# Linear attention: K^T V by heads in column strips, epsilon sums on ScalarE, second statistics moved behind the splits

## What is computed

```python
Q = relu(x @ Wq.T + bq) * decay      # (b, h, n, d), d = 32
K = relu(x @ Wk.T + bk) * decay
V = x @ Wv.T + bv
KV = einsum('bhnd,bhne->bhde', K, V)
Ksum = K.sum(axis=2)
Z = 1.0 / (einsum('bhnd,bhd->bhn', Q, Ksum)[..., None] + 1e-6)
out = einsum('bhnd,bhde->bhne', Q, KV) * Z
return out @ Wo.T + bo
```

## Time and profile before

| | |
|---|---|
| median of 3 runs | 2439.28 us (2438.57 to 2439.76) |
| profiled execution | 2436.57 us, its span 2435.0 us |
| TensorE busy | 2372.1 us (97%) |
| VectorE busy | 1214.1 us (50%) |
| ScalarE busy | 824.4 us (34%) |
| GpSimd busy | 862.6 us (35%) |
| mean granted TensorE clock | 0.993 of full speed |
| linear attention in the span | about 1473 to 1957 us |

### The profile page before, as it was taken

One profiled execution on the slowest core, in us unless ns is written; L12 is line 12 of the kernel. 1 busy time (PEld: TensorE's weight loads), 2 busy tenths in 40 slices (PEclk: granted clock), 3 DMA queues, 4 the chain that ended last, 5 costly groups with the idle time before them and its releaser, 6 DMA issues. The chain is left out here.

```text
span 2435.0 us, 39858 instructions
## 1 busy us (share of the span) xinstructions
PE 2372.1 (97%) x12749; PEld 1783.5 (73%) x12749; DVE 1214.1 (50%) x2551; ACT 824.4 (34%) x1392; POOL 862.6 (35%) x1098
## 2 busy tenths in 40 slices
PE   9999999999999999999999996999999999999997
PEld 7887755555555557788888885888888888888886
DVE  4334577777777758422222207776764732222221
ACT  3222355555555543344444431011111222222221
POOL 2000256565665552233333334442425221222112
PEclk9999999999999999999999998999999999999999
DMA  8895354545445328512121104140404242222200
GB/s 285 282 300 183 109 131 111 142 119 124 118 119 137 100 86 295 139 35 52 34 52 34 40 30 160 36 172 21 152 34 153 89 109 53 52 52 52 58 29 35
DMA packets 265860, 262.55 MB, mean 108 GB/s; under 512 B 128051, under 2 KB 161843, under 8 KB 265269
## 3 DMA queue, kind: packets, MB, share of 16 engines
q1 hardware_dynamic: 250148, 218.44, 31.2%
q0 software_dynamic: 6128, 24.21, 3.2%
q10 hardware_dynamic: 9504, 18.88, 2.3%
HBM read 168.68 MB, written 92.27 MB: 107 GB/s over the span
## 5 line engine op out<-in xcount | busy, mean ns | idle before, releaser
L191 DVE CUSTOM_DVE_ANT_0 junk<-psum,causal 128x896 bf16<-128x896 f32 (+7 forms) x512 | 373.3, 751 | 163.2 <-PE psum L971 137.8
L1080 ACT ACTIVATE p_probs<-psum 128x512 f32<-128x512 f32 (+1 forms) x640 | 317.4, 555 | 269.0 <-PE psum L984 264.8
L1607 POOL TENSOR_TENSOR p_h_lo<-p_h,p_h_hi 128x512 fp32r<-128x512 f32 x128 | 164.3, 1284 | 303.5 <-ACT p_h_hi L1630 303.5
L984 PE MATMUL psum<-qst,kst 98*128 98x512 f32 (+3 forms) x768 | 220.8, 367 | 1.8 <-PEq L280 0.9
L871 POOL TENSOR_SCALAR_AFFINE_SELECT p_probs<-p_probs 128x128 f32<-128x128 f32 x512 | 140.7, 297 | 223.3 <-ACT p_probs L1080 221.0
L2394 ACT ACTIVATE p_h<-psum,ffn_b 128x512 f16<-128x512 f32 x128 | 88.0, 688 | 372.5 <-PE psum L1259 357.6
L2370 POOL CAST p_h<-p_h 128x512 fp32r<-128x512 f16 x128 | 85.0, 664 | 364.6 <-ACT p_h L2394 364.1
L971 PE MATMUL psum<-kst,qst 96*128 96x128 f32 (+3 forms) x720 | 207.7, 362 | 0.8 <-ACT p_probs L1080 0.8
L984 PEld LDWEIGHTS psum<-qst,kst 98*128 98x128 f32 x768 | 130.8, 189 | 106.1 <-DVE rowmax L191 42.7
L1656 PE MATMUL psum<-tern,p_h_hi 128*128 128x512 f32 x512 | 199.4, 390 | 2.5 <-POOL p_h_lo L1607 2.5
L1656 PE MATMUL psum<-tern,p_h_lo 128*128 128x512 f32 x512 | 199.3, 389 | 0.0
(11 more groups left out here) (260 smaller groups left out, 4902.5 us busy)
## 6 DMA issues: line engine op xcount, KB each, us to landing
qst<-q_parts SPq DMA_DIRECT2D x96, 256.0 KB, 4.8
kst<-k_parts SPq DMA_DIRECT2D x96, 256.0 KB, 6.8
q_parts<-p_qk_out SPq DMA_DIRECT2D x32, 512.0 KB, 3.7
k_parts<-p_qk_out SPq DMA_DIRECT2D x32, 512.0 KB, 3.4
v_rows<-p_v_out SPq DMA_DIRECT2D x32, 256.0 KB, 4.4
v<-v_rows SPq DMA_DIRECT2D x16, 512.0 KB, 4.1
attention_out<-p_o_out SPq DMA_DIRECT2D x32, 256.0 KB, 2.1
p_x<-in_x SPq DMA_DIRECT2D x8, 1024.0 KB, 6.7
```

The lines of the kernel that those rows point to most:

```text
L191: return dve.tensor_tensor_reduce(view(junk[:, 0:n]), bank, view(self.causal[:, SEQ - n:SEQ]), 1.0, FLOOR, ALU.add, ALU.max, self.rowmax[: ...
L984: mm = pe.matmul(psum[:, bank, col:col + CH - q0], kst[s][0:KD + 2, g, j * P:(j + 1) * P], qst[s][0:KD + 2, c, g, q0:CH], start=True, stop ...
L1080: act.activation(probs[:, n % 2, g, col:CH], psum[:, banks_of(s, "s", st)[0], col:CH], ACT.Exp, scale=SM_SCALE).then_inc(p_ready, 1)
L1607: pool.tensor_tensor(h_lo[:, m % 2, :], h[:, m % 2, :], f32(h_hi[:, m % 2, :]), ALU.subtract).then_inc(hl_done, 1)
```

## The change

- `vs` holds V by tile, group and head in 33 columns: 32 of V and one of ones. K^T V is done head by head: 32 stationary columns of K by 33 moving ones, written to the head's 32 partitions of the bank, so that the four heads of a group use four column strips of the array. Per batch 128 matmuls stand in place of 32.
- TensorE waits for seven V tiles before K^T V, and for the eighth at the eighth tile of group 0.
- `same_head` and `kv` have the heads 33 columns apart; one VectorE multiply, which reads the bank's 33 columns four times over, makes `kv` of a group.
- Epsilon is added by ScalarE (Identity with a bias tile `eps`), half by half, into `den`; VectorE waits for it, takes the reciprocal, and scales a half in one multiply of 256 elements.
- In the last batch ScalarE's fifth weight piece comes behind the splits.
- In the loop, the statistics of the next batch's second chunk move from ahead of K^T V's eviction to behind the splits, and its normalization from there to behind the splits of the next batch's first chunk.
- The set-up on GpSimd has nine steps in place of twelve.

```diff
-        vs = sb("p5_v", [P, TT, GROUPS, P + 2], F32)
+        vs = sb("p5_v", [P, TT, GROUPS, HPG, HD + 1], F32)
...
+        eps = sb("p5_eps", [P, 1], F32)
+        heads_33 = lambda ap: ap.rearrange("p (a e) -> p a e", e=HD + 1)
...  ScalarE
                     if last:
-                        next_hi()
+                        next_hi(0, KT)
+                    for t in range(TT):
+                        if t >= 2:
+                            act.wait_ge(den_inv, 8 * b + t - 1)
+                        for half in range(2):
+                            A.wait_full(act, b, a_o(t, half))
+                            act.activation(den[:, t % 2, half * 2 * HPG:(half + 1) * 2 * HPG], heads_33(A.bank(a_o(t, half))[:, 0:2 * EXT])[:, :, HD],
+                                           ACT.Identity, bias=eps[:, 0:1]).then_inc(den_eps, 1)
                     for c in range(2):
                         part_hi(b, c, a_oT)
+                    if last:
+                        next_hi(KT, KT + 1)
...  TensorE
-                    pe.wait_ge(v_done, 8 * b + 8)
+                    pe.wait_ge(v_done, 8 * b + 7)
                     for g in range(GROUPS):
                         m = a_kv(g)
                         free_a(b, m)
-                        A.fill(partials(pe, A.bank(m)[:, 0:P + 2], [(ks[:, t, tok(g)], vs[:, t, g, :]) for t in range(TT)]), m)
+                        for t in range(TT):
+                            if g == 0 and t == TT - 1:
+                                pe.wait_ge(v_done, 8 * b + 8)
+                            for h in range(HPG):
+                                col = g * P + h * HD
+                                mm = pe.matmul(A.bank(m)[h * HD:(h + 1) * HD, 0:HD + 1], ks[:, t, col:col + HD], vs[:, t, g, h, :],
+                                               start=(t == 0), stop=(t == TT - 1))
+                        A.fill(mm, m)
...  VectorE
-                        if not last:
-                            ln_a.find_statistics(dve, 2 * b + 2 + c, x2_tile(c))
                         if c == 0 and not last:
+                            ln_a.find_statistics(dve, 2 * b + 2, x2_tile(0))
                             ln_a.normalize_tiles(dve, 2 * b + 2, x2_tile(0), x2_tile(0))
...
-                        dve.tensor_tensor(kv[:, g, 0:P], bank[:, 0:P], same_head[:, 0:P], ALU.mult)
-                        dve.tensor_scalar(kv[:, g, P:EXT], same_head[:, P:EXT], bank[:, P:P + 1], None, ALU.mult).then_inc(kv_done, 1)
+                        dve.tensor_tensor(heads_33(kv[:, g, :]), bank[:, None, 0:HD + 1].to_broadcast([P, HPG, HD + 1]), heads_33(same_head[:, :]),
+                                          ALU.mult).then_inc(kv_done, 1)
...
-                        for half in range(2):
-                            A.wait_full(dve, b, a_o(t, half))
-                            dve.tensor_scalar(slot(den)[:, half * 2 * HPG:(half + 1) * 2 * HPG].rearrange("p (g h) -> p g h", g=2),
-                                              halves[half][:, :, P:EXT], LIN_EPS, None, ALU.add).then_inc(den_eps, 1)
                         dve.wait_ge(den_eps, 16 * b + 2 * t + 2)
                         dve.reciprocal(slot(rden), slot(den)).then_inc(den_inv, 1)
...
                         for half in range(2):
-                            for g in range(2):
-                                at = (2 * half + g) * P
...
+                            at = 2 * half * P
+                            inv = slot(rden)[:, half * 2 * HPG:(half + 1) * 2 * HPG]
+                            A.wait_full(dve, b, a_o(t, half))
+                            dve.tensor_tensor(o_tok[:, t, at:at + 2 * P].rearrange("p (a e) -> p a e", e=HD), halves[half][:, :, 0:HD],
+                                              inv[:, :, None].to_broadcast([P, 2 * HPG, HD]), ALU.mult).then_inc(o_done, 1)
...
                     if not last:
-                        ln_a.normalize_tiles(dve, 2 * b + 3, x2_tile(1), x2_tile(1))
+                        ln_a.find_statistics(dve, 2 * b + 3, x2_tile(1))
...
                         if c == 0 and not last:
                             part_lo(b + 1, 0, a_x, 0)
+                            ln_a.normalize_tiles(dve, 2 * b + 3, x2_tile(1), x2_tile(1))
```

More of the change, by code:

```diff
@@ L1921, in _ @@
                 build(1, pool.memset(same_head[:, :], 0.0))
-                for g in range(HPG):
-                    build(2 + 2 * g, pool.memset(same_head[g * HD:(g + 1) * HD, g * HD:(g + 1) * HD], 1.0))
-                    build(3 + 2 * g, pool.memset(same_head[g * HD:(g + 1) * HD, P + g:P + g + 1], 1.0))
-                build(10, pool.memset(vs[:, :, :, P:P + 2], 1.0))
-                build(11, pool.memset(ident16[:, :], 0.0))
-                build(12, pool.affine_select(out=ident16[:, :], in_=ident16[:, :], compare_op=ALU.not_equal, fill=1.0, base=0,
+                for h in range(HPG):
+                    build(2 + h, pool.memset(same_head[h * HD:(h + 1) * HD, h * (HD + 1):(h + 1) * (HD + 1)], 1.0))
+                build(6, pool.memset(vs.rearrange("p t g h e -> p (t g h) e")[:, :, HD:HD + 1], 1.0))
+                build(7, pool.memset(eps[:, :], LIN_EPS))
+                build(8, pool.memset(ident16[:, :], 0.0))
+                build(9, pool.affine_select(out=ident16[:, :], in_=ident16[:, :], compare_op=ALU.not_equal, fill=1.0, base=0,
                                              pattern=[[-1, P]], channel_multiplier=1))
@@ L1971, in _ @@
                 act.wait_ge(consts_loaded, 16 * 6)
+                act.wait_ge(built, 7)
                 def body(b, last):
@@ L1979, in body, with next_hi @@
                         load_x1(act, b + 1, 0)
-                    def next_hi():
-                        for n in range(KT + 1):
+                    def next_hi(first, to):
+                        for n in range(first, to):
                             act.wait_ge(raw_loaded[n], 16)
@@ L2116, in body @@
                         if c == 0 and last:
-                            pe.wait_ge(built, 12)
+                            pe.wait_ge(built, 9)
                             pe.wait_ge(x_cast, 1)
@@ L2168, in _ @@
                         part_lo(0, 0, a_x, 0)
-                dve.wait_ge(built, 10)
+                dve.wait_ge(built, 7)
                 dve.wait_ge(consts_loaded, 16 * 6)
@@ L2183, in values @@
                             B.wait_full(dve, b, b_v(c, t))
-                            heads = lambda ap: ap.rearrange("p (g e) -> p g e", g=GROUPS)
-                            dve.tensor_tensor(vs[:, CT * c + t, :, 0:P], heads(B.bank(b_v(c, t))), heads(bias[:, 1, :]), ALU.add).then_inc(v_done, 1)
+                            heads = lambda ap: ap.rearrange("p (a e) -> p a e", e=HD)
+                            to = vs[:, CT * c + t, :, :, :].rearrange("p g h e -> p (g h) e")[:, :, 0:HD]
+                            dve.tensor_tensor(to, heads(B.bank(b_v(c, t))), heads(bias[:, 1, :]), ALU.add).then_inc(v_done, 1)
                     def next_lo(first, to):
```

8 lines of the change are left out of this document (2 added, 6 removed).

## The result

| | before | after |
|---|---|---|
| time, us (median, lowest to highest) | 2438.93 (2435.93 to 2439.76) | 2418.81 (2417.21 to 2422.34) |
| ratio, with 95% interval | 1 | 0.9922 [0.9905, 0.9939] |
| span of the profiled execution, us | 2435.0 | 2415.6 |
| mean granted clock of it | 0.993 | 0.992 |

The change saves 20.1 us by the medians. 25.9 had been forecast: the time is 5.4 us above the predicted 2413.4, inside the range. The interval of the ratio lies clear of 1.

The account below looks back on a forecast made before the run. TensorE, busy 97% of the span, was taken as the bound, with VectorE pacing the o stage. Three batches at 5.1 + 1.7 = 6.8 and a last at 3.8 + 1.7 = 5.5 save 25.9 us: median 2413.4, range 2405 to 2431.

Parts of the forecast that it names:

- K^T V in strips: K^T V stage: 256 short passes, 0.08 us per unit, bring the o stage 5.1 us earlier per loop batch, 3.8 in the last.
- The unit: K^T V: one token tile and group, two sets of four 33-column strip passes, taken as 0.08 us, lower end 0.07.
- The floor of 27 ns: Rival, chance 0.20: each K^T V strip matmul takes at least 27 ns, so 2.9 us saved per batch, 2427.7.
- the feed of 55 ns: Rival, chance 0.12: each K^T V matmul with its load costs 55 ns, kv takes 14.1 us, slower than before: 2456.5.
- The o stage, net 1.7: Q times kv, eight tiles: epsilon on ScalarE and wider multiplies, 8.8 us instead of 10.6, net 1.7 us per batch.
- ScalarE's round trip: Rival, chance 0.08: the o stage's loop stays at 2.7 us for two tiles, the 1.7 us are lost: 2420.2.
- Moved statistics cost nothing: Batch's end: statistics of 3.0 us fit in 3.4 us on VectorE behind the splits; cost nothing, 0.4 us to spare.
- The last batch's VectorE: Last batch: weight split and cast hold VectorE until 1908.34, so kv can't be evicted sooner; 3.8 us saved there.

Follow-up runs that it names:

- the kernel with the moved cast: Changed kernel; in the last batch alone, strips of tiles 0 to 3 precede V projections one group each, VectorE's third weight split and cast follow the splits: 2414.30 us.
- both paddings: Changed kernel with 64, then 128 semaphore increments ahead of the phase's first wait on TensorE's queue: 2436.69 us (one run) and 2429.36 us.

## Why the prediction was right, and where it was off

- **K^T V in strips, 5.1 us per loop batch.** Right in batches 2 and 3: the first reciprocal came 5.49 us earlier against 5.0 (5.1 less ScalarE's 0.1). The strips are 4.44 of it, and 1.05 the early start and the single multiply. The unit cost 0.072 instead of 0.08, 0.2 us over 25 units; from the last strip to the first 128-wide matmul it was 0.12, about the 0.1 allowed (1676.50 to 1676.63), but the last eviction didn't wait for it. The floor of 27 ns and the feed of 55 ns are both false here: 9 ns per pass, over 200 passes. The floor of about 25 ns between starts that the prediction cited from the Trainium skill ("TensorE: Matmul & The Clock Gate", "Wait — 56ns, not 53.3ns?") does not hold for four column strips in these traces.
- **The same term in batch 1 and in the last, wrong.** This is nearly the whole miss. The prediction priced the strips as if 256 passes could be issued as fast in every batch, and took its evidence, and the earlier trace rows, from code already run. The feed rival had the right kind of doubt (can the train be fed?) in the wrong form: not a slower rate per matmul, but one stop of 2 us. Batch 1 lost 2.35 us at the first reciprocal and 1.1 in the o stage by the clock. The last lacks 1.95 of its 5.5, and the kernel with the statistics moved back divides it: its code for the last batch is the same, its hole too (2.0 us), but the clock did not fall, and the next phase came 48.11 us after V's last eviction instead of 49.34. So 1.2 are the clock's, some 0.4 the hole's, and the remaining 0.3 the mis-sized o stage below. In the first batch, too, the fall was no certain part of the loss: it came behind four of nine such holes.
- **The o stage, net 1.7.** Mis-sized: 1.28 from first reciprocal to split, less 0.10 ahead of it. Two tiles take 2.36 us, not 2.28: ScalarE's eight elements 0.27 instead of 0.22, and its second half waits for the next TensorE passes. The old form also was quicker than 10.6 by 0.06. The gain came from the multiplies; the step to ScalarE, priced as a part of it, is worth 0.1. The rival "ScalarE's round trip" was near the truth in kind.
- **Moved statistics cost nothing.** Right. After the splits VectorE still waits 0.46 us for the residual's DMA (0.4 to spare was reckoned), and TensorE has no idle time at the batch's end. Undoing the move costs 1.37 per batch.
- **The last batch's VectorE.** Right that split and cast set the first kv eviction: 3.95 after V's, as before. That cover is also why its hole costs only some 0.4 directly: three evictions were over at 1893.2, and the fourth began at 1893.58, behind the hole. The clock took three times as much (1.2).
- **Errors that offset.** In batches 2 and 3 the kv part was 0.5 better and the o stage 0.5 worse than forecast, so 6.76 against 6.8 flatters the steps: that it fits to 0.04 is luck. The forecast as a whole stands because strips, multiplies and moved statistics work as it said; what the supply of code took, which it had put at nothing, was small beside them.

## What to carry to other kernels

Ask of each short, fast train of instructions not only what one costs, but whether its code has run before: a block of 256 instructions that is over sooner than the next one takes to come (mostly 3.2 to 3.9 us here, 128 small passes in 1.15) leaves TensorE idle, with "issue" as the only trace of it. If a stage gains in the loop's later turns but not in the first one and in a peeled last one, compare those turns row by row before any other explanation. And count the blocks that a loop touches: here 64 harmless instructions ahead of a loop made it fetch all its code again each turn, and by the count a few tens more inside it would do the same (not tried).

## What the runs showed of the hardware

- In four column strips a weight load of 128 by 32 and its matmul of 33 columns are issued every 9 ns, and with 17 columns as well.
- TensorE's loop of 1584 instructions ran without fetches over 7 blocks of 256 and with fetches in every turn over 8 (49 and 67 packets of the instruction queue in all, none against nine in a turn; 6.4 us more in the second turn, 3.3 in the third).
- From entering a block to running the next one took 3.2 to 3.9 us at 16 holes, 4.2 and 5.2 at two beside heavy DMA traffic (shares 0.67 and 0.75 until the packet came; that the traffic is the cause is not shown); the packet's record lies 2.3 to 2.9 us before the end of it.
- A semaphore increment on TensorE's queue takes 0.16 us (128 of them 20.6).
- An insertion of 32 strip passes between matmuls of 512 columns, with the waits in front of it, costs 0.3 us beyond the passes.
- After a hole of 2 us in the first batch the clock fell to the 1.2 GHz level in four profiles (the changed kernel twice, epsilon on VectorE, the kernel with the moved cast) and stayed at 2.4 in five (strips in the loop only, both paddings, statistics moved back, 17 columns); a fall cost 0.9 to 1.1 us of that batch. After the hole of the last batch it fell in six of seven profiles (not with the statistics moved back), and cost 1.2 in the changed kernel. Which of the two comes is not settled by these runs.
